# Second attention of a small language-model tower in 64x64 tiles of the tensor array, with the order of four engines drawn again

## The reference

```python
x = _rms_norm(x, gamma)
qkv = x @ w_qkv + b_qkv                 # 8 heads of 64
q = q * SCALE
a = jax.nn.sigmoid(x @ w_a + b_a)
a_cum = _safe_cumprod(a, axis=-2)
q = q * a_cum
k = k * (1.0 / jnp.maximum(a_cum, EPS_INV))
sim = jnp.einsum('bhid,bhjd->bhij', q, k)
attn = jnp.where(causal_mask, 0.0, sim)  # no softmax: keys up to the query
out = jnp.einsum('bhij,bhjd->bhid', attn, v)
return out.transpose(0, 2, 1, 3).reshape(b, n, DIM_INNER) @ w_out + b_out
```

## Time and profile before

| | |
|---|---|
| median of 3 runs | 390.12 us (389.3 to 391.22) |
| the profiled execution | 388.26 us |
| its span, first to last instruction | 386.3 us |
| PE busy | 354.4 us, 92% |
| DVE busy | 285.7 us, 74% |
| ACT busy | 214.4 us, 55% |
| POOL busy | 120.5 us, 31% |

### The profile page before, as it was taken

How to read it: one execution, slowest core, us unless ns; L and a number is a source line. 1 busy time by engine, 2 the same in 40 slices (tenths; PEclk the granted TensorE clock), 3 DMA queues, 4 the chain that set the end, 5 groups by cost and what they waited for, 6 DMA issues and landing times. The chain is left out here.

```text
span 386.3 us, 8686 instructions
## 1 busy us (share of the span) xinstructions
PE 354.4 (92%) x2701; PEld 274.4 (71%) x2701; DVE 285.7 (74%) x901; ACT 214.4 (55%) x480; POOL 120.5 (31%) x127
## 2 busy tenths in 40 slices
PE   3799678898999999999999999989997899999996
PEld 2668566485536995359855579654887799899996
DVE  1768868889999994988768899799854574325356
ACT  1258486774559635462337334673226675677680
POOL 7853111300015010300100147255521177377700
PEclk9999999999999999999999999998998999999999
DMA  5699999000000000000000085001112212341172
GB/s 135 204 411 365 296 292 276 5 3 2 0 0 3 3 2 0 2 1 2 2 0 3 0 266 214 15 16 42 34 41 56 58 43 79 83 132 56 35 249 82
DMA packets 25027, 33.87 MB, mean 88 GB/s; under 512 B 4674, under 2 KB 19786, under 8 KB 24600
## 3 DMA queue, kind: packets, MB, share of 16 engines
q1 hardware_dynamic: 22200, 27.49, 23.1%
q0 software_dynamic: 2784, 5.84, 4.7%
HBM read 19.10 MB, written 14.40 MB: 87 GB/s over the span
## 5 line engine op out<-in xcount | busy, mean ns | idle before, releaser
L1297 ACT ACTIVATE ht<-bank,arena 128x128 f32<-128x128 f32 x156 | 43.8, 368 | 14.3 <-PE bank L1037 11.0
L1048 PE MATMUL bank<-big,ht 128*128 x312 | 39.9, 278 | 1.2 <-ACT ht L1297 1.1
L744 POOL DMA_INDIRECT dealt<-xy,arena x32 | 32.7, 1022 | 24.6 <-DVE arena L1668 15.3
L1048 PEld LDWEIGHTS bank<-big,ht 128*128 128x128 f32 x312 | 36.9, 192 | 2.6 <-issue 2.3
L752 POOL DMA_INDIRECT experts_out<-arena x27 | 28.4, 1051 | 20.2 <-DVE arena L1777 13.2
L943 PE MATMUL bank<-xT_f,wq 128*128 128x512 f32 x64 | 30.9, 624 | 0.2 <-DVE vv L1547 0.2
L717 POOL TENSOR_TENSOR xn_d<-xn_d,wide 128x512 f32<-128x512 f32 x4 | 5.9, 1484 | 71.9 <-DVE wide L1500 71.9
L734 POOL TENSOR_TENSOR arena<-arena 128x8 f32<-128x8 f32 x4 | 6.7, 1669 | 56.0 <-DVE arena L1591 45.6
L1556 DVE TENSOR_TENSOR_SCAN lb<-la 128x512 f32<-128x512 f32 x16 | 21.6, 1352 | 0.7 <-PE bank L980 0.7
L943 PEld LDWEIGHTS bank<-xT_f,wq 128*128 128x128 f32 x64 | 11.9, 195 | 14.2 <-issue 11.1
L1577 DVE TENSOR_TENSOR arena<-bank,causal 128x512 f32<-128x512 f32 x32 | 20.1, 681 | 1.1 <-PE bank L972 0.5
(11 more groups left out here) (310 smaller groups left out, 891.1 us busy)
## 6 DMA issues: line engine op xcount, KB each, us to landing
dealt<-w1s SPq DMA_DIRECT2D x3, 1768.5 KB, 16.2
big<-in_tv SPq DMA_DIRECT2D x2, 2048.0 KB
big<-in_ew SPq DMA_DIRECT2D x16, 256.0 KB, 6.1
dealt<-w1s SPq DMA_DIRECT2D x2, 1572.0 KB, 21.5
arena<-dealt SPq DMA_DIRECT2D x27, 65.5 KB, 1.8
wq<-in_wq SPq DMA_DIRECT2D x1, 1024.0 KB, 16.8
vv<-experts_out SPq DMA_DIRECT2D x2, 512.0 KB, 5.1
out<-h SPq DMA_DIRECT2D x3, 256.0 KB, 2.2
```

Of the source, the lines that this page charges most:

```text
L744: pool.indirect_dma_start(xs, bass.IndirectOffsetOnAxis(ap=goal[b][:, k, t:t + 1], axis=0), xy[b % 2][:, k, t, :], None).then_inc(s_deal[b ...
L1048: last = pe.matmul(p[:, 0:D], hid[n % DEEP][:, c * P:(c + 1) * P], big[:, bass.ds(e * FF + (E * FF + c * D), D)], start=(c == 0), stop=(c ...
L1297: last = act.activation(hid[n % DEEP][:, c * P:(c + 1) * P], of("K.up", n)[:, c * P:(c + 1) * P], ACT.Gelu, bias=eb1[:].rearrange("p e c - ...
```

## The change

- QK and AV are done in 64x64 tiles. The later half of a chunk's keys meets the later half of its queries only. A product of early or late keys is one matmul: the 64 keys that meet all 128 queries in 128 columns ("wide", new line 973), the 64 that meet the late queries in 64 columns ("narrow", line 977). The bank holds 2 x 192 columns instead of 512, and the mask is applied to 384.
- So that four tiles can be used, the two token halves of every chunk change places in the keys of odd pairs (`halves`), in the decay that multiplies them, and in the values; the rows of `wo1` for odd pairs are rolled by 64.
- AV has two banks for each chunk (`G.av0`, `G.av1`), by pair parity. Its matmuls: early keys (`new_low`, line 992, wide), state (`old`, line 1004), late keys (`new_high`, line 998, narrow). PE waits for two semaphores of its own: "low" before the second half of the state matmuls, "old" before the last late-key matmuls.
- V is four matmuls of 256 columns on two 128x64 tiles for each former one (line 940).
- ACT copies the AV result in two pieces (line 1307).
- The strings of ORDER are new for PE, ACT, DVE and POOL; the phases in them are the same.

```diff
     "pe": (
-        "N0.0 N1.0 N2.0 T0.3 N3.0 T0.5 N4.0 T0.7 A0.2 T1.3 T1.5 N5.0 N6.0 N7.0 N8.0 N9.0 T1.7 N10.0 N11.0 N12.0 "
...
+        "N0.0 N1.0 N2.0 T0.3 T0.5 N3.0 T0.7 N4.0 A0.2 T1.3 N5.0 N6.0 T1.5 T1.7 N7.0 N8.0 N9.0 N10.0 A1.2 N11.0 N12.0 "
...
+        side = [slice(0, HALF), slice(HALF, P)]
+        def halves(tokens, j):
+            view = tokens.rearrange("p (c h t) -> p c h t", c=T, h=2)
+            return view[:, :, ::-1] if j % 2 else view
...
                     for t in range(T):
                         p = room(pe, "F.v%d" % t, b)
                         wait(pe, "F.act.xT", b)
-                        did(pe.matmul(p[:], xT_f[:, t * P:(t + 1) * P], wq[:, 2 * 512:3 * 512], start=True, stop=True),
-                            "F.pev.v%d" % t, b)
+                        for k in range(2):
+                            for half in range(2):
+                                last = pe.matmul(p[side[half ^ k], :].rearrange("p (g k c) -> p k g c", g=2, k=2)[:, k],
+                                                 xT_f[:, t * P + half * HALF:t * P + (half + 1) * HALF],
...
-                            did(pe.matmul(p[:], wq[:, at * 512 + j * P:at * 512 + (j + 1) * P], xT_f[:], start=True, stop=True),
+                            did(pe.matmul(halves(p[:], 0), wq[:, at * 512 + j * P:at * 512 + (j + 1) * P],
+                                          halves(xT_f[:], at * j), start=True, stop=True), "F.peq.%s%d" % (name, j), b)
...
-                    for j in range(PAIRS):
-                        wait(pe, "F.dveq.k%d" % j, b)
-                        for m in range(2):
-                            rows = slice(m * HD1, (m + 1) * HD1)
-                            last = pe.matmul(half[m][:, j * P:(j + 1) * P], kk[rows, j, tk], qq[rows, j, tk],
-                                             start=True, stop=True)
...
+                    for g in range(2):
+                        at = g * SIMW
+                        for j in (2 * g, 2 * g + 1):
+                            wait(pe, "F.dveq.k%d" % j, b)
+                            for m in range(2):
+                                pe.matmul(half[m][side[j % 2], at:at + P], kk[side[m], j, (low, high)[j % 2]], qq[side[m], j, tk],
+                                          start=True, stop=True)
+                        for j in (2 * g, 2 * g + 1):
+                            for m in range(2):
+                                last = pe.matmul(half[m][side[1 - j % 2], at + P:at + SIMW], kk[side[m], j, (high, low)[j % 2]],
+                                                 qq[side[m], j, high], start=True, stop=True)
...
+                    def new_low(j, m):
+                        g, r = j // 2, j % 2
+                        return pe.matmul(part[r][side[m ^ r], g * P:(g + 1) * P],
+                                         vv[side[r], c, (2 * j + m) * HD1:(2 * j + m + 1) * HD1], sim[k][side[r], m, g, 0:P],
...
+                    def new_high(j, m):
+                        g, r = j // 2, j % 2
+                        return pe.matmul(part[r][side[m ^ r], g * P + HALF:(g + 1) * P],
+                                         vv[side[1 - r], c, (2 * j + m) * HD1:(2 * j + m + 1) * HD1],
...
+                    def old(j, m):
+                        g, r = j // 2, j % 2
+                        return pe.matmul(part[r][side[m ^ r], g * P:(g + 1) * P],
+                                         ss[(n - 1) % 2][side[m], j, side[m]], qq[side[m], j, tk],
...
+                    for g in range(2):
+                        new_low(2 * g, 1)
+                        last = new_low(2 * g + 1, 0)
+                        if g == 1:
+                            did(last, "G.pe2.low", n)
+                        new_low(2 * g, 0)
+                        last = new_low(2 * g + 1, 1)
+                    if c == 0:
+                        did(last, "G.pe2.old", n)
+                    else:
+                        wait(pe, "S.act2.s", state(n - 1))
+                        for g in range(2):
+                            old(2 * g, 0)
+                            last = old(2 * g + 1, 1)
+                        did(last, "G.pe2.old", n)
+                    wait(pe, "G.pe2.low", n)
+                    for g in range(2 if c else 0):
+                        old(2 * g + 1, 0)
+                        old(2 * g, 1)
+                    for g in range(2):
+                        new_high(2 * g, 1)
+                        new_high(2 * g + 1, 0)
+                    wait(pe, "G.pe2.old", n)
+                    for g in range(2):
+                        new_high(2 * g, 0)
+                        last = new_high(2 * g + 1, 1)
...
-                    did(act.activation(oc[k][:].rearrange("p a b -> p (a b)"), of("G.av", n)[:], ACT.Copy), "G.act.o", n)
+                    for i in range(2):
+                        did(act.activation(oc[k].rearrange("p (g i) c -> p i g c", i=2)[:, i],
+                                           of("G.av%d" % i, n)[:, 0:2 * P].rearrange("p (g c) -> p g c", g=2), ACT.Copy),
+                            "G.act.o%d" % i, n)
...
-                                              causal[:].unsqueeze(1).to_broadcast([P, PAIRS, P]), ALU.mult), "G.dve.m%d" % m, n)
+                                              causal[:].unsqueeze(1).to_broadcast([P, 2, SIMW]), ALU.mult), "G.dve.m%d" % m, n)
```

More of the change, by code:

```diff
@@ L104 @@
     "G.pe": ["qk0", "qk1"],
-    "G.pe2": ["av"],
+    "G.pe2": ["low", "old", "av"],
     "G.pe3": ["out"],
-    "G.act": ["o"],
+    "G.act": ["o0", "o1"],
     "S.pe": ["tr"],
@@ L285, in lm_tower @@
         kt = [take([P, PAIRS, P]) for i in range(2)]
-        sim = [take([P, 2, PAIRS, P]) for i in range(2)]
+        spare = [take([P, 2 * S]) for i in range(2)]
+        sim = [x[:, 0:2 * 2 * SIMW].rearrange("p (m g c) -> p m g c", m=2, g=2) for x in spare]
         oc = [take([P, PAIRS, P]) for i in range(2)]
@@ L966, in section_G @@
                 if ph == 4:
-                    p = room(pe, "G.av", n)
+                    part = [room(pe, "G.av%d" % i, n) for i in range(2)]
+                    def new_low(j, m):
+                        g, r = j // 2, j % 2
+                        return pe.matmul(part[r][side[m ^ r], g * P:(g + 1) * P],
+                                         vv[side[r], c, (2 * j + m) * HD1:(2 * j + m + 1) * HD1], sim[k][side[r], m, g, 0:P],
+                                         start=(g == 0), stop=False, skip_group_check=True)
@@ L1871, in lay @@
     a["gam"] = g["gamma"].reshape(P, 1)
[L1873 removed]
+    low = np.triu(np.full((HALF, P), HD1 ** -0.5, np.float32))
+    a["causal"] = np.tile(np.concatenate([low, low[:, 0:HALF]], axis=1), (2, 1))
     m = {k[7:]: np.asarray(v) for k, v in i.items() if k.startswith("L1_ffn_")}
```

49 lines of the change are left out of this document (24 added, 25 removed), and 92 rows, old and new, of the table ORDER.

## The result

| kernel | median, us | lowest to highest | runs | ratio to before, 95% interval |
|---|---|---|---|---|
| before | 389.71 | 388.85 to 391.22 | 4 | |
| after | 376.25 | 375.26 to 380.22 | 4 | 0.966 [0.961, 0.971] |
| after, again beside variants | 373.33 | 372.13 to 377.61 | 6 | 0.960 [0.955, 0.966] |

What follows compares the result with a forecast made beforehand. PE's own work was taken to bound the second attention (120 to 290 us); 3.5 + 9.6 + 0.6 = 13.7 us less of it, at 96% busy, gains 11 us: 379 us forecast, range 374 to 388.

Steps and rivals of the forecast that it cites:

- PE sets the pace in the stretch: Second attention (120 to 290 us): PE's work sets the pace; 13.7 us less of it, at 96% busy, gains 11 us.
- the first rival: Second attention: DVE late more often, PE's share 93%, 6 us gained, 384 us; chance 0.15, with dear narrow passes.
- Four tiles at once, and the scores: QK blocks: four 64x64 tiles run at once; a block takes 0.66 us for 0.88, 3.5 us less over 16.
- two at a time: QK and AV: only two 64x64 tiles run at once; 12 us slower, 402 us; chance 0.06.
- issue: QK and AV: no pass follows another faster than 55 ns; 26 us slower, 416 us; chance 0.04.
- AV of later chunks at 1.24: AV blocks of chunks 1 to 3: 1.24 us for 2.04, self-waits covered by queued state matmuls; 9.6 us less over 12.
- self-waits open: AV: both waits of PE on itself stop it a full pass; 8.6 us come back, 388 us; chance 0.08.
- Changes of shape: PE's tile-shape changes: 69 become 53; 4 fewer beyond those counted in AV, 0.6 us less.
- V at no cost but the changes of shape: V projection: four matmuls on two column tiles cost the same as before, except tile-shape changes in and out, four times.
- The ring of banks: PSUM ring of seven banks: AV uses 16 more places; DVE and ACT have slack in all windows but one.
- The tables: Redrawn order tables, outside the stretch: same steps in nearly the same succession; 0, and 2 us either way.
- Nothing for the clock: Granted clock, 0.99 of 2.4 GHz in the stretch: PE stays at least some nine tenths as full, so nothing counted.

Runs made afterwards that it cites:

- after, again beside variants: The changed kernel itself measured once more, unchanged, on the same chip as three variants of it, as their base: 373.33 us, 0.960 of the kernel before.
- the run with the old tables: The changed code with the four order tables of the kernel before put back, all else of the change kept: 390.79 us, ratio 1.002 to before.

## Why the prediction was right, and where not

**PE sets the pace in the stretch: right, with luck in the sum.** Scores and AV cost PE 9.0 us less (45.4 to 36.4) and V 0.1 more a block; the stretch with its exit to the experts got 9.4 shorter. The two are near each other because several things cancel: PE's idle time in the stretch grew from 3.4 to 5.9 us, the exit lost 1.8, and the lower clock in the trace of before gave at least 1.3. PE's share was 95.1%, forecast 96%. From 250 to 270 us PE was busy for 14.8 of 20 us only (17.8 before), and 4.1 us of its waits there were for DVE, busy for 18.3 (92%). So DVE sets the pace in that window, as the first rival had it; over the stretch it did not take over, with 138.5 of the 170 us, 81%.

**Four tiles at once, and the scores: right.** 0.68 us a block for 0.66; the passes of 64 columns cost 0.055 of pitch and not 0.11. Both slow rivals (two at a time, issue) are out: an AV block of 48 passes took 1.44 us, 30 ns a pass. The prediction applied the Trainium skill's rule (TensorE: Matmul & The Clock Gate, "Back-to-back issue gap"), some 62 ns for each matmul with hardware decode off, to passes. An fp32 matmul is two passes, so by that rule the block's 24 matmuls would take 1.5 us, an estimate. That is near the 1.44 measured, and neither this block nor the 55 ns a pass of before decides. The scores do: 16 matmuls in 0.68 us are 42 ns each, and the late half's 8 in 0.23 are 29. The trace does not agree with a floor of 62 ns; whether hardware decode was off, no run here shows.

**AV of later chunks at 1.24: wrong.** The step that failed is that the two waits of PE on itself cost nothing if 0.44 us of state matmuls are already queued. Behind such a wait the first pass starts 0.34 us after the last awaited one, with the state matmuls of the other column half running in between, so the queued work did not cover it. It cost 3.1 us in all, 0.2 a block; the prediction's own sign for it, PE idle behind its own semaphores, is in the row of L998's weight loads above. AV of chunk 0 went the same way: 1.01 us without a change of shape, where 0.86 was forecast. What is left of the later blocks, about 0.13 each, is in the 0.50 us that four-tile halves took for 0.44. All AV blocks were to lose 9.6 us and lost 6.7 (29.1 to 22.4). The rival "self-waits open" had the mechanism and overpriced it: 8.6 us, as if each stopped the whole array for a full pass.

**Changes of shape: right.** The V block with one more behind it is 0.14 us longer, and the traces count 16 fewer changes in the whole program, as forecast.

**Mask and copy: right.** 550 ns for 548, 381 for 384.

**V at no cost but the changes of shape: right in size.** 3.60 us a block for 3.46.

**The ring of banks: named, and passed over.** "DVE and ACT have slack for that" asked for an engine's slack where the place in the ring decides. In the old order the same edit leaves 7.9 us of idle PE in front of AV, about as much as the tiles gain.

**The tables: wrong.** The term outside the stretch, 0 and 2 us either way, was in truth 3 to 4.5 us, all in the expert part; and inside the stretch the forecast treated the new order as no term at all, while without it the tiles are worth nothing. That the sum came out near is luck in part: 11 us forecast; 9.1 from tiles and attention order, 3 to 4.5 from the end.

**Nothing for the clock: not quite.** The granted clock moved by itself between runs of one kernel, and with it the time by about 3 us (last section).

## What to carry to other kernels

When a change makes a step take one more buffer of a ring, list for that step who holds the buffer that it will get, and when that reader ends; a mask of a later chunk or a slow small product can hold it, and the profile may call the wait "issue". A faster block in an in-order queue needs its queue drawn again, and the two should be priced together and the order also alone. As far as these runs show, split products over row groups that add into one bank only if the order leaves the wait between them, per column half, something of its own to do. Look at the granted clock of each stretch before you explain a difference of 1 to 3 us between two traces.

## What the runs showed of the hardware

- Four 64x64 tiles take their first passes within 0.04 us, 7 ns apart in the trace, and a block of 48 such passes runs at 30 ns a pass.
- Passes of fp32 matmuls in different tiles don't stand in the program's order in the trace: a matmul's second pass starts behind the first passes of matmuls that follow it in other tiles. In after, two passes of the next block's L992 start at 144.17, and the last two of this block's L998 at 144.19.
- A product of 8 columns on DVE took 1.1 to 1.3 us while POOL ran an elementwise operation of 512 columns (1.27 us), and 0.23 otherwise (L1492 in the run with the old tables and in after).
- Matmuls of another row group into the same bank and columns, behind a semaphore of PE's own, begin 0.34 us after the start of the last awaited pass.
- The two runs of the changed kernel differ by 3.5 us of span, 3.0 of it ahead of the first scores, where the granted clock from 40 to 80 us was 0.91 in one and 1.00 in the other. The first is after, the second the same kernel again:

```profile
40.00:80.00 40.00, 33.63 (x215) 25.33 (x216) 31.73 (x98) 25.49 (x48) 6.49 (x6) 0.91 0.75 204
```

```profile
40.00:80.00 40.00, 33.55 (x225) 23.88 (x223) 34.45 (x99) 28.17 (x50) 7.57 (x6) 1.00 0.72 200
```

What lowers the clock was not looked into; it is at the lower of its two levels, 1.2 GHz, for some of the time. At the same granted clock the two sets agree: at 0.986 one run of each is 374.9 and 374.8 us long. So medians of this kernel taken at different times shouldn't be compared more closely than 3 us. A single block compares well where the clock is 1.00 in both traces; a whole stretch can be 1 to 4 us off, as shown above.
